# One barrier per token block in place of waits on single counters, in an eight-core layer kernel

## The reference

```
xn = layernorm(x)
# attention, per head and sequence, blocks of 32 tokens:
low = mean_block(Q) @ mean_block(K).T * SCALE        # 64 x 64 block scores
norm = low - rowmax(low) + band * 5000
thresh = the 1024th largest of norm;  hi_mask = norm >= thresh
hi = exact attention in the kept blocks;  low part for the rest
# feed-forward:
xr = mu_r*xn + (1-mu_r)*shift(xn);  xk = mu_k*xn + (1-mu_k)*shift(xn)
out = sigmoid(xr @ W_r.T) * (relu(xk @ W_k.T)**2 @ W_v.T)
x = x + attention + feed_forward
```

## Time and profile before

| | |
|---|---|
| median of 3 runs | 5608.54 us (5603.25 to 5619.15) |
| profiled execution | 5614.01 us, span of the slowest core 5612.4 us |
| spans of the eight cores | 5570.1 to 5612.4 us |
| busy share of the span | PE 56%, DVE 44%, ACT 30%, PEld 20%, POOL 5% |
| chain that ended last | PE 36%, DVE 22%, DMA 15%, ACT 14%, issue 11% |

### The profile page before, as it was taken

How to read it: one execution, slowest core, us unless ns; L and a number is a source line. 1 busy time by engine, 2 the same in 40 slices (tenths; PEclk the granted TensorE clock), 3 DMA queues, 4 the chain that set the end, 5 groups by cost and what they waited for, 6 DMA issues and landing times.

```text
span 5612.4 us, 57690 instructions; the slowest of 8 cores (5570.1 to 5612.4 us)
## 1 busy us (share of the span) xinstructions
PE 3127.1 (56%) x11513; PEld 1107.5 (20%) x11513; DVE 2487.4 (44%) x5263; ACT 1708.7 (30%) x2627; POOL 306.6 (5%) x343
## 2 busy tenths in 40 slices
PE   1114434212222435777776776776776777777676
PEld 0012222101111111222222222222222222122122
DVE  3432232215555323643653652752752752653653
ACT  2300000000000001453454454354354355355255
POOL 0000000010000000000000000000000000000000
PEclk9998666656665776787797787788788788789688
DMA  1143332100110221100100110110110110110100
GB/s 62 61 77 85 74 67 50 26 21 21 32 30 23 55 58 25 33 18 12 34 18 16 29 23 16 25 27 16 23 29 14 25 29 12 27 27 6 29 20 18
DMA packets 517452, 181.72 MB, mean 32 GB/s; under 512 B 494954, under 2 KB 496146, under 8 KB 516946
## 3 DMA queue, kind: packets, MB, share of 16 engines
q1 hardware_dynamic: 482386, 130.46, 10.3%
q0 software_dynamic: 34752, 47.57, 4.6%
HBM read 142.23 MB, written 39.34 MB: 32 GB/s over the span
## 4 chain that ended last, share of the span: by engine, by line
PE 36%; DVE 22%; DMA 15%; ACT 14%; issue 11%; DVEq 1%; ACTq 1%; POOL 0%; SPq 0%; POOLq 0%
PE pS L898 9%; DVE bm L824 8%; ACT aT L913 7%; PE pO L866 7%; PE pA L813 7%; PE pA L1059 4%; PE pA L531 3%; PE pA L1120 2%; DMA fW<-wT_r 2%; ACT stage L994 2%; DMA fW<-wT_k 2%; DMA fW<-wT_v 2%; DMA nb<-norm_all 2%; DVE fA L516 2%; DVE bis_ge L421 1%
## 5 line engine op out<-in xcount | busy, mean ns | idle before, releaser
L824 DVE TENSOR_REDUCE bm<-pA 128x16 f32<-128x512 f32 x1664 | 1150.9, 692 | 602.4 <-PE pA L813 472.1
L913 ACT ACTIVATE aT<-pS 128x1024 bf16<-128x1024 f32 x1024 | 1048.8, 1024 | 771.9 <-PE pS L898 729.2
L866 PE MATMUL pO<-aT,vtm 128*65 128x512 bf16 x2048 | 704.7, 430 | 306.8 <-ACT aT L913 306.2
L813 PE MATMUL pA<-ktp,qtp 64*128 64x512 bf16 x1664 | 683.8, 422 | 307.6 <-ACT aT L913 107.6
L898 PE MATMUL pS<-rhsc,lhsc 128*128 128x512 bf16 x2048 | 718.3, 439 | 0.2 <-issue 0.2
L531 PE MATMUL pA<-fA,fW 128*128 128x512 bf16 x1536 | 406.0, 421 | 499.2 <-DVE fF L653 144.4
L866 PEld LDWEIGHTS pO<-aT,vtm 128*65 128x65 bf16 x2048 | 236.2, 123 | 644.9 <-issue 496.6
L824 DVE TENSOR_REDUCE bm<-pO 128x16 f32<-128x512 f32 x384 | 265.5, 691 | 210.8 <-PE pO L813 177.9
L813 PEld LDWEIGHTS pA<-ktp,qtp 64*128 64x128 bf16 x1664 | 152.6, 95 | 875.6 <-issue 872.0
L531 PEld LDWEIGHTS pA<-fA,fW 128*128 128x128 bf16 x1536 | 154.2, 106 | 744.4 <-issue 624.2
L610 ACT ACTIVATE fR<-pA 128x512 bf16<-128x512 f32 x64 | 38.2, 597 | 785.8 <-PE pA L531 777.4
(11 more groups left out here) (150 smaller groups left out, 2472.7 us busy)
## 6 DMA issues: line engine op xcount, KB each, us to landing
xtile<-x SPq DMA_DIRECT2D x64, 512.0 KB
fW<-wT_r SPq DMA_DIRECT2D x64, 256.0 KB
fW<-wT_k SPq DMA_DIRECT2D x64, 256.0 KB
fW<-wT_v SPq DMA_DIRECT2D x64, 256.0 KB
out<-stage SPq DMA_DIRECT2D x32, 512.0 KB
rhsc<-qtp POOLq DMA_DIRECT2D x32, 256.0 KB, 3.5
lhsc<-ktp POOLq DMA_DIRECT2D x32, 256.0 KB, 2.9
bx<-bsm_dram POOLq DMA_DIRECT2D x32, 256.0 KB, 7.5
```

What stands on the lines that cost most here:

```text
L813: e.matmul(pap, qtp[p0:p0 + 64, ts0 + t * 128:ts0 + (t + 1) * 128], ktp[p0:p0 + 64, ts0 + kq * 512:ts0 + (kq + 1) * 512], start=True, stop ...
L824: e.tensor_reduce(bmp[:, kq * 16:(kq + 1) * 16], pap.rearrange("p (k e) -> p k e", e=32), axis=AX.X, op=ALU.max))
L866: e.matmul(pO[0:65, sl * 512:(sl + 1) * 512], vtm[:, (sq * 16 + k) * 130 + hip * 65: (sq * 16 + k) * 130 + hip * 65 + 65], aT[bpar][:, sl ...
L913: e.activation(aT[bpar][:, :], pS[bpar][:, :], AF.Exp, scale=0.125))
```

## The change

Four things are edited. At the end of each of the eight blocks, after its last site, all engines now meet at a barrier. The two places where DVE waited for TensorE's whole count before the first mix of a block are gone. `prev_dma` and `prev_add` start at zero in every block, so that nothing of the block before is waited for. In `emit_sel_b` TensorE no longer waits for ACT's count before it transposes.

```
@@ emit_sel_b
                 r.wait("tensor", "sDV", ndv_s)
-                r.wait("tensor", "sAC", r.cnt["sAC"])
                 npe_s = r.emit("tensor", lambda e: e.transpose(
                     pB1s[0:64, 0:64], sel_buf[:, :], id_f[0:64, 0:64]))
@@ the loop over blocks
             wpd_load("q", 0)
             wpd_load("q", 1)
-            prev_dma = [0, 0]
-            prev_add = [0, 0]
             r.wait("vector", "sPE", r.cnt["sPE"])
             for Q in range(8):
                 t0 = Q * QT
-                r.wait("vector", "sPE", r.cnt["sPE"])
                 mu_mix(fA, "r", t0)
...
                 r.wait("tensor", "sDV", r.cnt["sDV"])
+                prev_dma = [0, 0]
+                prev_add = [0, 0]
                 for tt in range(QT // 128):
...
                 do_site(Q * 3 + 2)
+                r.barrier()
             emit_sel_post()
             r.barrier()
```

## The result

The changed kernel took 5623.11 us (median of 19 runs, 5612.11 to 5654.13) against 5609.15 us for the kernel before (19 runs, 5599.20 to 5619.48): a ratio of 1.0032, 95% interval 1.0022 to 1.0042. That is 18 us by the ratio, 12 to 24 by its interval, against 5.8 forecast. The time lies in the range that was given, and the direction is right; the size was three times too small, and the rest of this document is mostly about the part that was missing. In some runs of any kernel the cores of one half of the chip (0 to 3 or 4 to 7) show a lower granted clock and take longer, so for the experiments I also give the quicker half, which is the mean span of the four cores of the half with the shorter one, as a median over the runs.

The account below looks back on a forecast made before the run. Bound: a relay between DVE and TensorE in the second stage, neither saturated. Barrier +11.0, mask transposes -3.95, row tiles -1.3 gave +5.8 us, on the median 5608.5 making 5614 us; range 5601 to 5629.

Parts of the forecast that it names:

- The barrier at the first two block ends: Second stage: the next block's first mix waits for POOL's last weight load to land, 5.5 and 5.2 us.
- The row on the landing of this very load: Profile rows giving POOL's weight-slice load 4.1 and 4.0 us to land, used instead of the skill page's 3.2 us.
- The third to the seventh block: Block ends where POOL's last row-tile store lands before the site's work ends; barrier waits already met, costed at nothing.
- the barrier in a row: Rival: barrier waits looked at one after another, 1 us at each of eight ends; +16 us, 5625, chance 0.08.
- The eighth block: Second barrier before `emit_sel_post`; stores already landed, SP has three more counters to look at: 0.3 us.
- The mask transposes and row tiles: Second stage: `emit_sel_b` saves 0.10 us a step plus 0.85 at site 21, -3.95; earlier first tile copies, -1.3 us.
- The sum of the second stage: Barrier 11.0, mask transposes -3.95, row tiles -1.3, removed DVE waits 0: +5.8 us.
- what it adds or takes there arrives at the end one for one: Premise: second-stage changes reach the end unaltered, as the unedited third stage (3,491 of 5,612 us) starts behind a barrier.
- unknown costs: Part of the range: +2 to +12 us on the median 5608.5, with about 8 us of median spread on either side.
- rival on the clock of the third stage: Slowest core draws a granted clock 0.003 lower, 5629 us, chance 0.10; or 0.003 higher, 5599, chance 0.05.
- a difference within 0.3%: No change by the measurement's bound of about 0.3%, 16.8 us; times 5592 to 5625, chance 0.83.
- the 0.14: Chance of slower by over 0.3%, above 5625 us: the lower-clock case and half of the one-after-another barrier waits.

Follow-up runs that it names:

- the barrier alone: Kernel before with the eight block-end barriers added and nothing taken out; ratio 1.0025 (1.0004 to 1.0045).
- DVE's old length: Changed kernel less ten DVE waits at the barriers, covered by others, so DVE's stream is as long as before; ratio 1.0022, 5603.93 us.
- the kernel without the gates: Changed kernel without the barrier at the first two block ends, old TensorE wait and tile counts kept there; ratio 1.0011 (0.9994 to 1.0028).
- the lean version: Kernel before without TensorE's waits for ACT in `emit_sel_b` and for old tile copies, no block barrier, stream lengths kept; ratio 0.9986, 5596.83 us.

## Why the prediction was right, and where it fell short

**The barrier at the first two block ends**: right in mechanism and size. Forecast 5.5 and 5.2 us; mean gaps over eight cores 5.51 and 5.54, intervals +5.2 and +6.1, and +11.2 for the pair when put in alone. The row on the landing of this very load (4.0 and 4.1 us) was the right one to use: with the estimate of 3.2 us from the Trainium skill (DMA: Bandwidth & Descriptors, Anatomy of one DMA) the pair would have been 9.0, which the measured 11 does not bear out. Within the two blocks nothing gave the wait back. The shorter intervals later in the stage (the fifth block and the end of the stage, some 7 us together with the barrier alone) were in no term of the sum.

**The third to the seventh block**: right. The mixes follow after 0.16 to 0.24 us instead of 0.11 to 0.14, some 0.4 us for all five, and no store is waited for. The rival of the barrier in a row, which needed 1 us at each of them, falls by that.

**The eighth block**: 0.3 us was forecast; DVE's last mask copy ends at 2083.35 and the mask store goes out at 2083.63 on core 1, a gap of 0.28 where it was 0.16 on that core before. Right within 0.2 us.

**The mask transposes and row tiles**: right. 0.10 us a step, the sigmoid no longer waited for, 1.62 us to the first tile copy; the mask steps by their intervals 4.0 us, against 3.95. The 4.8 us of the kernel without the gates, against 5.2 for both terms, hold some of the unexplained 4 us as well and are no confirmation of the sum.

**The sum of the second stage**: +4.5 on the first pair of profiles, +3.4 with DVE's old length, against the kernel before on another chip (the medians of the kernel before on the two are 5598.02 and 5597.95), where +5.8 was forecast. That it comes so close is in part luck: each term was found where it was put, but the late intervals shrank beside them.

**What failed** is the sentence ahead of all terms: "what it adds or takes there arrives at the end one for one", since the third stage "is not edited". It is not edited, but it is moved. DVE's stream has ten entries more ahead of it, and that alone makes the third stage 12 to 22 us longer. With 14.5 us in the third stage the sum would have been +20.3, against a measured 18. That 5623 lies in the range is luck as well: unknown costs were given up to +12 us, which ends at 5620.5, and only the 8 us added for a median's spread reach further. The forecast's own rival on the clock of the third stage named the right place, a granted clock lower by 0.003 and +15 us (the mean of the eight cores went from 0.775 to 0.771 between the two profiles), and called it a draw of chance. It is not: it repeats with the length of DVE's stream on the three chips of the experiments, and goes when the length is restored. That rival had 0.10, and should have been argued from the program, with the counts of instructions of each engine ahead of the unedited stage.

The chances put 0.83 on a difference within 0.3%; the estimate is 1.0032, so it fell just beyond, in the 0.14.

## What to carry to other kernels

Price a barrier by the DMA that is in flight where it falls: it costs the landing of the last one less the work that was going to cover it, at each place by itself, and nothing where that work is longer. A wait that has long been met cost 0.10 us on TensorE where it stood behind the one that holds, so redundant waits in a ping-pong between two engines are worth counting. Before a difference of a few tenths of a percent is put on an edit, run the old kernel with as many waits added, met at once, as the edit adds: what moves then is the place of the unedited instructions. And compare the quicker half of the chip beside the slowest core: here that showed the gain of the lean version, which the ratio of the times left open.

## What the runs showed of the hardware

DVE leaves 0.46 us or somewhat less instead of 0.10 between two of its operations at some entries of its stream, waits counted, and these lie a multiple of 128 apart: all 14 such gaps of the third stage in the kernel before and all 16 in the changed one stand at remainder 52 or 53 of the entry's number by 128. ACT has gaps of 0.37 us at remainder 17 or 18. In a loop whose chain runs over DVE, ten entries more ahead of it changed a stage of 3,477 us by 12 to 22 us on three chips, while 32 entries on ACT changed it by 2 and 32 each on SP and POOL by 4, the quicker half by 1.1 at most. The granted clock of the last 330 us went from 0.83 or 0.84 to 0.81 or 0.82 with it. The second stage of the kernel before differed by 10 us between its two profiles, its third by less than 1. A load of 128x1024 elements from f32 to bf16 that POOL issues landed after 4.0 to 4.7 us.
